# Holding GpSimd's gathers away from the slot products of a DLRM interaction kernel

## Chip, cores and metric

One NeuronCore of a Trainium2 chip. The metric is the device time of one execution in microseconds; the kernel before takes 124.73 us (median of 3 runs, 124.36 to 125.06).

## The reference, cut to what matters

512 samples, 26 embedding tables (1000 to 125000 rows of 128 floats) and one dense vector of 128 floats per sample. Per sample there are 27 slots (dense and 26 table rows); all 351 products of two different slots, with the dense vector twice, go through a three-layer MLP.

```python
e = jnp.stack([tbl_0[ids[:, 0]], ..., tbl_25[ids[:, 25]]], axis=1)
combined = jnp.concatenate((dense_features[:, None, :], e), axis=1)
interactions = jnp.einsum('bfd,bgd->bfg', combined, combined)
interactions_flat = interactions[:, iu, ju]          # 351 pairs, iu < ju
z = jnp.concatenate((dense_features, interactions_flat), axis=1)
h = jnp.concatenate([z, dense_features], axis=1)
h = jnp.maximum(h @ W_top1 + b_top1, 0.0)            # 607 -> 512
h = jnp.maximum(h @ W_top2 + b_top2, 0.0)            # 512 -> 256
y = h @ W_top3                                       # 256 -> 1
```

## The kernel before, in words

**Two ways to look up.** The 11 smallest tables are loaded whole into SBUF, and TensorE looks their rows up by multiplying with 0/1 masks (`look_up_first`, `look_up`, lines 321 to 365). The other 15 tables stay in HBM: GpSimd fetches their rows with indirect DMAs, one per table and tile of 128 samples, so 4 x 15 = 60 gathers (line 313), each of 128 rows of 512 bytes. The buffer `emb` holds two tiles. Gathers of tiles 1 and 2 fill it; those of tiles 3 and 4 take the places of tiles 1 and 2, once TensorE has transposed what was there (`s_tr`).

**The order of the gathers.** They go out one after the other, tile by tile. GpSimd does nothing else then. The function `hold(t, i)` (line 283) puts a wait ahead of gather `i` of tile `t`, `t` counted from 0; in this text tiles are counted from 1, as the loop over `p` does, and gathers of a tile from 0 to 14. Groups 0 to 3 of a tile (`GROUPS`) are its gathers 0 to 3, 4 to 7, 8 to 11 and 12 to 14, and each group has a semaphore (`s_gather`).

**The loop.** After the lookups, TensorE runs `Fori(1, TILES + 1)` over the tiles. What it does in iteration `p`, in program order:

- slot products, first half (`products`, line 408): for each of 16 column sets and each of 4 quarters of the array one 27 x 27 product of `xT` with itself, in float32. The profile shows two matmul records and two weight loads for each product, so 128 matmul records a half;
- `turn_next(p, (0,))`: transposes of group 0 of tile `p + 1` (line 374), 4 records; in iteration 1 also `dense_part` (line 414);
- slot products, second half, at whose end `s_prod` is incremented;
- for `p` over 1 the last layer of the tile before (`result`, line 445) and `dense_part`; then `turn_next(p, (1,))`, the transposes of group 1;
- `turn_pairs` (line 421) and the first layer (line 414), with VectorE's and ScalarE's rearranging of the products in between (lines 585 to 596 and 693 to 696);
- `turn_next(p, (2, 3))`, the transposes of groups 2 and 3, 7 records, then the second layer (line 504, 16 records).

Each transposed group is packed into `xT` by VectorE or ScalarE (lines 515 and 619), and the next iteration's products wait for that (`s_ready`). TensorE works through this order strictly: while it waits for a group of gathers, everything listed behind it waits too.

```python
                products(range(MATMULS // 2))
                turn_next(p, (0,))
                with nc.tensor.If(p < 2):
                    dense_part(slice(0, P), (0, 1))
                products(range(MATMULS // 2, MATMULS)).then_inc(s_prod, 1)
```

Of the kernel before, what the change touches and what calls it, by code (L numbers as in the profile page):

```python
# [46 lines left out]

QUADS = 4
MATMULS = P // QUADS


HALF = (SLOTS - 1) // 2
# [18 lines left out]
def build(nc, dense_t, ids, spread_ids, pair_ids, other_ids, resident, gathered, weights, out):  # L71
# [5 lines left out]
    first_step = [sum(n_rows[p[0]] for p in PAIRS[:b]) for b in range(len(PAIRS) + 1)]  # L77
# [7 lines left out]
    with ExitStack() as ctx:  # L85
        def sb(name, shape, dt=F32):
            return ctx.enter_context(nc.sbuf_tensor(name, shape, dt))

        def sem(name):
            return ctx.enter_context(nc.semaphore(name))  # L90
# [14 lines left out]
        known = sb("known", [D, 1 + RESIDENT, BATCH])  # L105
        xT = sb("xT", [D, MATMULS, QUADS, SLOT_PITCH])
        inter_s = sb("inter_s", [P, SLOTS * (ROW_PITCH + 1) + 1])
# [10 lines left out]

        prod = ctx.enter_context(nc.psum_tensor("prod", [P, MATMULS, SLOT_PITCH], F32))
        half_bank = [prod[:, h * MATMULS // 2:(h + 1) * MATMULS // 2, :].rearrange("p j g -> p (j g)")  # L120
                     for h in range(2)]
# [31 lines left out]
        s_used = sem("s_used")  # L153
# [7 lines left out]
        s_tr = sem("s_tr")  # L161
        s_pack = [sem(f"s_pack{g}") for g in range(NG)]
        s_prod = sem("s_prod")
        s_blk = sem("s_blk")
        s_wrap = sem("s_wrap")
        s_pick = [sem(f"s_pick{k}") for k in range(K_TILES)]
# [2 lines left out]
        s_l1 = sem("s_l1")  # L169
# [73 lines left out]
        def rows(t, c):  # L243

            return emb[:, t % 2 * GATHERED + c, :]

        def w1_pairs(k):
            return w_sb[0:K_PAIRS, W1P + k * HID1:W1P + (k + 1) * HID1]
# [26 lines left out]
        @block.gpsimd  # L275
        def _(pool):
            nc.gpsimd.memset(ident[:], 0.0).then_inc(s_zero, 1)
            pool.wait_ge(s_zero, 1)
            nc.gpsimd.affine_select(out=ident[:], in_=ident[:], compare_op=ALU.not_equal, fill=1.0, base=0,
                                    pattern=[[-1, P]], channel_multiplier=1).then_inc(s_ident, 1)  # L280
            pool.wait_ge(s_ids, 16)

            def hold(t, i):


                if (t, i) == (1, 0):
                    pool.wait_ge(s_used, first_step[2])
                if (t, i) == (1, 8):
                    pool.wait_ge(s_used, first_step[3] + 2)
                if (t, i) == (2, 0):  # L290
                    pool.wait_ge(s_used, first_step[4] + 3)
                if (t, i) == (2, 6):
                    pool.wait_ge(s_used, first_step[5] + 3)
                if (t, i) == (2, 10):
                    pool.wait_ge(s_prod, 1)
                if (t, i) == (3, 0):
                    pool.wait_ge(s_l1, 2)
                if (t, i) == (3, 4):
                    pool.wait_ge(s_prod, 2)
                if (t, i) == (3, 9):  # L300
                    pool.wait_ge(s_l1, 4)
                if (t, i) == (3, 13):
                    pool.wait_ge(s_prod, 3)

            for t in range(TILES):
                for g, (first, n) in enumerate(GROUPS):
                    if t >= 2:

                        pool.wait_ge(s_tr, NG * (t - 2) + g + 1)
                    for c in range(first, first + n):  # L310
                        hold(t, c)
                        i = t * GATHERED + c
                        nc.gpsimd.indirect_dma_start(  # L313
                            out=rows(t, c), out_offset=None, in_=gathered[c],
                            in_offset=bass.IndirectOffsetOnAxis(ap=ids_sb[:, i:i + 1], axis=0),
                        ).then_inc(s_gather[t % 2][g], 16)

        @block.tensor
        def _(pe):
# [83 lines left out]
            def products(some):  # L403

                for i in some:
                    for q in range(QUADS):
                        x = xT[:, i, q, 0:SLOTS]
                        mm = nc.tensor.matmul(prod[SLOT_PITCH * q:SLOT_PITCH * q + SLOTS, i, 0:SLOTS], x, x,  # L408
                                              start=True, stop=True)
                return mm  # L410
# [12 lines left out]
            def dense_part(samples, some):  # L423
                for n in some:
                    layer1(n, w1_sum, known[:, 0, samples], False)
# [39 lines left out]
            with nc.tensor.Fori(1, TILES + 1) as p:  # L465


                pe.wait_ge(s_ready, 2 * p)

                products(range(MATMULS // 2))  # L470
                turn_next(p, (0,))
                with nc.tensor.If(p < 2):
                    dense_part(slice(0, P), (0, 1))
                products(range(MATMULS // 2, MATMULS)).then_inc(s_prod, 1)
                samples = bass.ds((p - 1) * P, P)
                with nc.tensor.If(p > 1):

                    result(p - 1)
                    dense_part(samples, (0, 1))
                turn_next(p, (1,))  # L480

                pe.wait_ge(s_kept_last, 1)
                pe.wait_ge(s_y, p)
                turn_pairs(p, 0)
                dense_part(samples, (2, 3))
                pe.wait_ge(s_pair[0], p)
                first_pairs((0, 1))
                turn_pairs(p, 1)
                turn_pairs(p, 2)
                first_pairs((2, 3))  # L490
                for n in range(HID1 // P):
                    for k in range(1, K_TILES):
                        if n == 0:
                            pe.wait_ge(s_pair[k], p)
                        mm = layer1(n, w1_pairs(k), pairs[0:K_PAIRS, k, :], k == K_TILES - 1)
                    if n % 2:
                        mm.then_inc(s_l1, 1)
                turn_next(p, (2, 3))
                for half in range(2):
                    pe.wait_ge((s_h1_act, s_h1_dve)[half], p)  # L500
                    for m in range(HID2 // P):
                        for c in (2 * half, 2 * half + 1):
                            first = W2 + c * HID2 + m * P
                            mm = nc.tensor.matmul(l2_bank[m][:, 0:P], w_sb[:, first:first + P], h1[:, c, :],  # L504
                                                  start=(c == 0), stop=(c == HID1 // P - 1))
                        if half:
                            mm.then_inc(s_l2, 1)
# [3 lines left out]
        def _(dve):  # L511
# [66 lines left out]
            for t in range(TILES):  # L578
# [5 lines left out]
                for rows in (slice(0, K_ROWS), slice(K_ROWS, SLOTS)):  # L584
                    nc.vector.transpose(blocks[:, rows, 0:MATMULS],  # L585
                                        prod[:, :, rows].rearrange("p j g -> p g j")).then_inc(s_blk, 1)
# [188 lines left out]
```

## Time and profile before

| | before |
|---|---|
| runs, median (lowest to highest) | 124.73 us (124.36 to 125.06) |
| span of the profiled execution, first to last instruction | 123.0 us |
| median of the runs less that span | 1.73 us |
| TensorE matmul busy | 104.2 us (85%) |
| GpSimd busy | 65.7 us (53%), of it the 60 gathers 65.0 us |
| chain that ended last | PE 83%, issue 13%, DVE 2%, ACT 1% |
| line 408, idle just before its matmuls | 14.7 us, of it "issue" 14.2 us |

The profiled execution's own time is given as its span alone. How to read it: the span is cut into engine busy time; a busy share is no bound by itself. "Issue" is time in which an engine waited for nothing that the profile shows. "PEclk" is the clock that TensorE was granted, as a share of 2.4 GHz.

### The profile page before, as it was taken

The page shows a single profiled execution, that of the slowest core. Times are in us where ns is not written, and L with a number is a line of the kernel's source. Part 1 is how long each engine was busy: PE and PEld are TensorE (multiplying, and loading weights), DVE is VectorE, ACT ScalarE, POOL GpSimd, SP SyncE. Part 2 cuts the span into 40 slices and gives each one's busy share as a digit, 9 for nine tenths or more (in the row PEclk, how much of TensorE's full clock was granted, in tenths as well). Part 3 has the DMA queues.
Part 4 walks back from the last instruction along what each step waited for, and adds up shares of the span by engine and source line. Part 5 has one row for each costly group of instructions (what it writes and reads, how often), then busy time and mean ns, then how long its engine had stood idle before and what let it go on. Part 6 is the DMA issues. An engine that isn't in the chain of part 4 may idle for free.

```text
span 123.0 us, 3436 instructions
## 1 busy us (share of the span) xinstructions
PE 104.2 (85%) x1516; PEld 87.9 (71%) x1516; DVE 65.4 (53%) x110; ACT 48.1 (39%) x81; POOL 65.7 (53%) x66
## 2 busy tenths in 40 slices
PE   6999999999999999962178996289995299998993
PEld 6787888888888888831067895177992278996991
DVE  2599999999899996820001742105540106451411
ACT  4542979197794931300000462002541102730321
POOL 3887888579878887877500887503778305000000
PEclk9999999999999999999555999756999558999999
DMA  3799999999211112121200111200112100000000
GB/s 57 236 400 365 402 398 408 410 392 368 80 43 45 45 43 48 44 63 43 64 5 5 43 43 43 64 0 0 45 43 64 43 0 20 23 0 0 0 0 1
DMA packets 3949, 13.51 MB, mean 110 GB/s; under 512 B 1315, under 2 KB 1317, under 8 KB 3302
## 3 DMA queue, kind: packets, MB, share of 16 engines
q1 hardware_dynamic: 2018, 9.48, 20.5%
q0 software_dynamic: 1920, 3.94, 11.2%
q8 instruction: 4, 0.07, 0.2%
q14 instruction: 3, 0.02, 0.1%
q10 hardware_dynamic: 4, 0.00, 0.0%
HBM read 13.42 MB, written 0.00 MB: 109 GB/s over the span
## 4 chain that ended last, share of the span: by engine, by line
PE 83%; issue 13%; DVE 2%; ACT 1%
PE bank L365 17%; PE prod L408 13%; PE bank L414 13%; PE prod L365 12%; PE bank L374 7%; PE bank L504 6%; PE prod L433 4%; PE bank L321 4%; PE bank L325 3%; PE bank L445 2%; DVE inter_s L585 1%; PE bank L438 1%; PE prod L421 1%; PE bank L421 0%; DVE xT L575 0%
## 5 line engine op out<-in xcount | busy, mean ns | idle before, releaser
L313 POOL DMA_INDIRECT emb<-in_tbl,ids_sb x60 | 65.0, 1083 | 38.3 <-PE prod L408 19.3
L522 DVE TENSOR_SCALAR mask<-ids_h,ids_sb 128x1024 fp32r<-128x1024 int16 (+1 forms) x48 | 31.5, 699 | 2.2 <-issue 0.8
L408 PE MATMUL prod<-xT 128*27 128x27 f32 x1024 | 16.8, 215 | 14.7 <-issue 14.2
L408 PEld LDWEIGHTS prod<-xT 128*27 128x27 f32 x1024 | 13.6, 128 | 18.8 <-issue 17.4
L585 DVE STREAM_TRANSPOSE inter_s<-prod 128x288 f32<-128x288 f32 (+1 forms) x8 | 4.6, 611 | 26.3 <-PE prod L408 26.3
L365 PE MATMUL bank<-mask,high 128*128 128x512 f32 x46 | 15.2, 393 | 0.0
L365 PE MATMUL bank<-mask,low 128*128 128x512 f32 x46 | 15.0, 390 | 0.0
L414 PE MATMUL bank<-pairs,w_sb 117*128 117x128 f32 x96 | 12.7, 282 | 0.1
L414 PEld LDWEIGHTS bank<-pairs,w_sb 117*128 117x128 f32 x96 | 11.6, 191 | 0.7 <-ACT pairs L696 0.5
L531 DVE TENSOR_TENSOR low<-table,high 128x1024 fp32r<-128x1024 f32 (+1 forms) x9 | 11.7, 1301 | 0.0
L374 PE MATMUL bank<-ident,emb 128*128 128x128 f32 x60 | 10.5, 310 | 0.9 <-issue 0.9
L635 ACT CAST high<-table 128x1024 fp32r<-128x1024 f32 (+1 forms) x9 | 9.7, 1132 | 2.6 <-PE bank L325 2.6
L365 PE MATMUL prod<-mask,high 128*128 128x512 f32 x32 | 10.0, 395 | 0.0
L365 PEld LDWEIGHTS bank<-mask,low 128*128 128x128 f32 x46 | 8.6, 188 | 1.8
L365 PE MATMUL prod<-mask,low 128*128 128x512 f32 x32 | 9.9, 390 | 0.0
L693 ACT COPY pairs_s<-inter_s 128x117 f32<-128x117 f32 x8 | 2.3, 291 | 19.2 <-DVE inter_s L585 17.4
L365 PEld LDWEIGHTS bank<-mask,high 128*128 128x128 f32 x46 | 8.5, 188 | 1.7
L374 PEld LDWEIGHTS bank<-ident,emb 128*128 128x128 f32 x60 | 8.0, 160 | 1.8 <-issue 1.3
L711 ACT COPY y_row<-bank 1x128 f32<-1x128 f32 x4 | 1.0, 254 | 19.3 <-PE bank L445 19.3
L504 PE MATMUL bank<-h,w_sb 128*128 128x128 f32 x64 | 8.0, 278 | 0.0
L504 PEld LDWEIGHTS bank<-h,w_sb 128*128 128x128 f32 x64 | 7.5, 192 | 0.2 <-issue 0.2
L611 DVE TENSOR_SCALAR h<-bank,ids_sb 128x128 f32<-128x128 f32 x4 | 1.4, 351 | 11.3 <-remote 8.7
(55 smaller groups left out, 118.1 us busy)
## 6 DMA issues: line engine op xcount, KB each, us to landing
table<-in_resident SPq DMA_DIRECT2D x3, 1024.0 KB
w_sb<-in_weights SPq DMA_DIRECT2D x1, 1792.0 KB
table<-in_resident SPq DMA_DIRECT2D x1, 1280.0 KB
table<-in_resident SPq DMA_DIRECT2D x4, 256.0 KB
emb<-in_tbl,ids_sb POOLq DMA_INDIRECT x60
ids_h<-in_other_ids SPq DMA_DIRECT2D x1, 896.0 KB
table<-in_resident SPq DMA_DIRECT2D x1, 640.0 KB
ids_h<-in_pair_ids SPq DMA_DIRECT2D x1, 256.0 KB
```

The lines of the kernel that those rows point to most:

```text
L313: nc.gpsimd.indirect_dma_start(out=rows(t, c), out_offset=None, in_=gathered[c], in_offset=bass.IndirectOffsetOnAxis(ap=ids_sb[:, i:i + 1] ...
L321: nc.tensor.matmul(looked(r), split(high, r)[:, k * D:(k + 1) * D], made(k)[:, r, :], start=(k == 0), stop=False)
L365: mm = nc.tensor.matmul(looked(r), split(part, r)[:, k * D:(k + 1) * D], made(step)[:, r % 2, :], start=(k == 0 and part is high), stop=(k ...
L374: mm = nc.tensor.transpose(group_bank(g)[:, i * P:(i + 1) * P], rows(t, first + i), ident[:])
L408: mm = nc.tensor.matmul(prod[SLOT_PITCH * q:SLOT_PITCH * q + SLOTS, i, 0:SLOTS], x, x, start=True, stop=True)
L414: return nc.tensor.matmul(l1_bank[n // 2][:, (n % 2) * P:(n % 2 + 1) * P], weights[:, n * P:(n + 1) * P], x, start=(weights is w1_sum and ...
L433: nc.tensor.matmul(half_bank[1][:, 0:WARM_COLUMNS], warm, warm[:, 0:WARM_COLUMNS], start=True, stop=True)
L504: mm = nc.tensor.matmul(l2_bank[m][:, 0:P], w_sb[:, first:first + P], h1[:, c, :], start=(c == 0), stop=(c == HID1 // P - 1))
L522: nc.vector.tensor_scalar(made(step)[:, 0:n, :], ids_h[:, 2 * b:2 * b + n, :], col_sb[:, row:row + 1], None, ALU.is_equal).then_inc(s_mask, 1)
L531: nc.vector.tensor_tensor(split(low, r), raw(r), split(high, r).bitcast(F32), ALU.subtract).then_inc(s_low, 1)
L585: nc.vector.transpose(blocks[:, rows, 0:MATMULS], prod[:, :, rows].rearrange("p j g -> p g j")).then_inc(s_blk, 1)
L635: nc.scalar.copy(split(high, r), raw(r)).then_inc(s_high, 1)
```

## The change

Five of the nine waits of `hold` go, three come, and one more semaphore, `s_quiet`, is incremented by TensorE once per iteration, when 4 of the 16 column sets of the second half are done (32 of its 128 matmul records). Gathers 4 to 10 of tile 3 go out after that point of iteration 1, gathers 11 to 14 of tile 3 and 0 to 3 of tile 4 after that point of iteration 2, and gathers 4 to 14 of tile 4 after that point of iteration 3.

```diff
+STIR = MATMULS // 2 + 4
...
+        s_quiet = sem("s_quiet")
...
-                if (t, i) == (2, 6):
-                    pool.wait_ge(s_used, first_step[5] + 3)
-                if (t, i) == (2, 10):
-                    pool.wait_ge(s_prod, 1)
-                if (t, i) == (3, 0):
-                    pool.wait_ge(s_l1, 2)
+                if (t, i) == (2, 4):
+                    pool.wait_ge(s_quiet, 1)
+                if (t, i) == (2, 11):
+                    pool.wait_ge(s_quiet, 2)
                 if (t, i) == (3, 4):
-                    pool.wait_ge(s_prod, 2)
-                if (t, i) == (3, 9):
-                    pool.wait_ge(s_l1, 4)
-                if (t, i) == (3, 13):
-                    pool.wait_ge(s_prod, 3)
+                    pool.wait_ge(s_quiet, 3)
...
-                products(range(MATMULS // 2, MATMULS)).then_inc(s_prod, 1)
+                products(range(MATMULS // 2, STIR)).then_inc(s_quiet, 1)
+                products(range(STIR, MATMULS)).then_inc(s_prod, 1)
```

GpSimd's instructions keep their order, only their waits move. The first place is tile 3's gathers 4 to 14 (in_tbl_7 is gather 4, in_tbl_23 gather 14; `s_tr` is the wait for the transposes that free the buffer, `s_used` one for a lookup step). Before:

```order
L313 DMA emb<-in_tbl_7,ids_sb 128x128 [waits s_tr]
L313 DMA emb<-in_tbl_9,ids_sb 128x128
L313 DMA emb<-in_tbl_11,ids_sb 128x128 [waits s_used]
L313 DMA emb<-in_tbl_14,ids_sb 128x128
L313 DMA emb<-in_tbl_17,ids_sb 128x128 [waits s_tr]
L313 DMA emb<-in_tbl_18,ids_sb 128x128
L313 DMA emb<-in_tbl_19,ids_sb 128x128 [waits s_prod]
L313 DMA emb<-in_tbl_20,ids_sb 128x128
L313 DMA emb<-in_tbl_21,ids_sb 128x128 [waits s_tr]
L313 DMA emb<-in_tbl_22,ids_sb 128x128
L313 DMA emb<-in_tbl_23,ids_sb 128x128
```

The same gathers on GpSimd in the change:

```order
L311 DMA emb<-in_tbl_7,ids_sb 128x128 [waits s_quiet,s_tr]
L311 DMA emb<-in_tbl_9,ids_sb 128x128
L311 DMA emb<-in_tbl_11,ids_sb 128x128
L311 DMA emb<-in_tbl_14,ids_sb 128x128
L311 DMA emb<-in_tbl_17,ids_sb 128x128 [waits s_tr]
L311 DMA emb<-in_tbl_18,ids_sb 128x128
L311 DMA emb<-in_tbl_19,ids_sb 128x128
L311 DMA emb<-in_tbl_20,ids_sb 128x128 [waits s_quiet]
L311 DMA emb<-in_tbl_21,ids_sb 128x128 [waits s_tr]
L311 DMA emb<-in_tbl_22,ids_sb 128x128
L311 DMA emb<-in_tbl_23,ids_sb 128x128
```

Seven gathers stand between the first wait for `s_quiet` and the second. The second place is tile 4's gathers 4 to 14 on GpSimd, before:

```order
L313 DMA emb<-in_tbl_7,ids_sb 128x128 [waits s_prod,s_tr]
L313 DMA emb<-in_tbl_9,ids_sb 128x128
L313 DMA emb<-in_tbl_11,ids_sb 128x128
L313 DMA emb<-in_tbl_14,ids_sb 128x128
L313 DMA emb<-in_tbl_17,ids_sb 128x128 [waits s_tr]
L313 DMA emb<-in_tbl_18,ids_sb 128x128 [waits s_l1]
L313 DMA emb<-in_tbl_19,ids_sb 128x128
L313 DMA emb<-in_tbl_20,ids_sb 128x128
L313 DMA emb<-in_tbl_21,ids_sb 128x128 [waits s_tr]
L313 DMA emb<-in_tbl_22,ids_sb 128x128 [waits s_prod]
L313 DMA emb<-in_tbl_23,ids_sb 128x128
```

And in the change:

```order
L311 DMA emb<-in_tbl_7,ids_sb 128x128 [waits s_quiet,s_tr]
L311 DMA emb<-in_tbl_9,ids_sb 128x128
L311 DMA emb<-in_tbl_11,ids_sb 128x128
L311 DMA emb<-in_tbl_14,ids_sb 128x128
L311 DMA emb<-in_tbl_17,ids_sb 128x128 [waits s_tr]
L311 DMA emb<-in_tbl_18,ids_sb 128x128
L311 DMA emb<-in_tbl_19,ids_sb 128x128
L311 DMA emb<-in_tbl_20,ids_sb 128x128
L311 DMA emb<-in_tbl_21,ids_sb 128x128 [waits s_tr]
L311 DMA emb<-in_tbl_22,ids_sb 128x128
L311 DMA emb<-in_tbl_23,ids_sb 128x128
```

Before, the wait at gather 4 was for the products of iteration 2; now it is for a point in those of iteration 3, and all eleven gathers stand behind that one wait.

## Rows read from the trace of the kernel before

**Rows 1.** The span and mean granted clock of the core.

```profile
core 0: 123.0 us, clock 0.902
```

**Rows 2.** The page's costliest groups: line 408's matmuls, and the idle time before them.

```profile
L408 PE MATMUL prod<-xT 128*27 128x27 f32 x1024 | 16.8, 215 | 14.7 <-issue 14.2
```

**Rows 3.** Windows of the slot products: stretch, length, PE busy (records), PEclk, DMA share, GB/s.

```profile
53.70:62.22 8.52, 2.37 (x57) 0.75 0.19 48
62.22:63.31 1.09, 1.09 (x72) 0.50 0.00 0
65.53:67.22 1.69, 1.64 (x128) 0.50 0.00 0
75.00:80.33 5.33, 1.56 (x40) 0.82 0.19 50
80.33:81.62 1.29, 1.29 (x90) 0.50 0.00 0
82.67:84.31 1.64, 1.64 (x129) 0.50 0.00 0
92.81:97.94 5.13, 1.36 (x31) 0.76 0.20 51
110.15:113.17 3.02, 2.47 (x256) 1.00 0.00 0
```

**Rows 4.** Windows behind each tile's products; busy: PE, PEld, DVE, ACT, POOL; clock, DMA.

```profile
67.22:75.00 7.78, 7.22 (x65) 6.92 (x69) 4.81 (x10) 3.97 (x9) 6.00 (x6) 0.94 0.16 44
84.31:92.81 8.50, 8.50 (x66) 7.41 (x64) 4.80 (x10) 4.32 (x10) 6.18 (x6) 0.95 0.15 40
102.31:110.15 7.84, 7.84 (x74) 7.35 (x75) 4.71 (x10) 4.50 (x11) 1.89 (x2) 1.00 0.06 17
113.17:123.00 9.83, 7.89 (x60) 6.52 (x59) 2.93 (x8) 2.42 (x9) 0.00 (x0) 0.99 0.00 0
```

**Rows 5.** The chain that ended last, in order of time: start, us, what.

```profile
53.70 0.52 PE prod L408 x38
54.23 0.18 issue
...
81.62 1.05 PE bank L374 x4
...
110.15 1.20 PE prod L408 x83
111.35 0.55 issue
111.90 1.27 PE prod L408 x83
```

**Rows 6.** GpSimd's timeline: start, us, and in brackets the idle time before.

```profile
51.88 0.94 POOL L313 DMA_INDIRECT emb<-in_tbl,ids_sb  x1 [0.30 <-issue]
...
59.37 0.94 POOL L313 DMA_INDIRECT emb<-in_tbl,ids_sb  x1 [0.30 <-issue]
67.48 0.94 POOL L313 DMA_INDIRECT emb<-in_tbl,ids_sb  x1 [7.17 <-PE prod L408]
...
75.59 0.94 POOL L313 DMA_INDIRECT emb<-in_tbl,ids_sb  x1 [0.30 <-issue]
...
78.08 0.94 POOL L313 DMA_INDIRECT emb<-in_tbl,ids_sb  x1 [0.30 <-issue]
```

**Rows 7.** The chain in iteration 3 behind its products.

```profile
103.47 0.44 PE bank L374 x4
...
107.60 0.77 PE bank L374 x7
108.36 1.79 PE bank L504 x16
```

**Rows 8.** Windows around the fall and the return of the granted clock in iteration 2.

```profile
78.00:79.00 1.00, 0.08 (x4) 0.10 (x4) 0.00 (x0) 0.00 (x0) 0.92 (x1) 0.70 0.24 66
...
85.00:86.00 1.00, 1.00 (x8) 0.86 (x8) 0.93 (x3) 0.60 (x3) 0.89 (x1) 0.89 0.00 0
```

## The prediction, made before the changed kernel ran

> **What bounds the kernel now.** I read the span first [rows 1]: 123.0 us, 1.73 below the median of the runs (124.73). I take 1.73 as what lies around every span. The costliest groups come next: line 408's 1024 matmul records are busy for 16.8 us, yet TensorE sat idle for 14.7 us just ahead of them, 14.2 of it "issue", with nothing in the profile that it waited for [rows 2]. The windows show where [rows 3]. A half of the products is 128 records. Iteration 4's two halves took 3.02 us in all, with no DMA traffic at all. Iteration 1 ran only 57 records in its first 8.52 us, iteration 2 only 40 in 5.33, iteration 3 only 31 in 5.13; each of these stretches has a DMA share of 0.19 or 0.20. The remaining records of the same halves, and all the second halves, ran without a break, and their rows have no DMA traffic.
>
> Only gathers were under way then. GpSimd's last one before the pause started at 59.37 and took 0.94, so it ended at 60.31, and TensorE ran freely from 62.22; in iteration 2 the last one ended at 79.02, and TensorE was free from 80.33, which is 1.31 later [rows 3, 6]. So it is the transfer, which ends behind the instruction, that matters. At the start of each stretch some records pass unhindered: 38 in iteration 1 before the first gap, at 54.23 [rows 5]. Something of that size stands ready ahead of the array; after it, the other 19 of the 57 took 8.0 us, 2.4 a microsecond. The long matmuls between the products, 66 records in 8.50 us with six gathers on GpSimd, show no idle time [rows 4]; that is 7.8 a microsecond, so what starves the products is not a fixed rate, and I only take from the rows when it starts and when it ends.
>
> The gaps cost twice. The clock was 1.00 in iteration 4's products and 0.50 behind each starved stretch [rows 3]: with a gap-ridden TensorE it fell near 78.7 (0.70 over 78 to 79) and came back near 85 (0.89 over 85 to 86) [rows 8].
>
> **The change, part by part.** All times are in the profiled span.
>
> *Iteration 1.* Products start at 53.70 as before. Tile 3's gather 3 (51.88 plus 0.94) goes as before, gather 4 is held. Its transfer is over by 54.1 (1.31 behind its end), just when the first gap came, so I leave 0.3 us of stall: first half 1.20 [rows 5] + 0.3 = 1.5. Between the halves stand four transposes and four `dense_part` records, 2.22 us from 63.31 to 65.53 at half clock [rows 3]; at full clock half of that, and 0.3 for the branches, which cost 0.55 where they stood alone [rows 5]: 1.4. Second half 1.27. Products end at 57.9 where it was 67.22. The rest of the iteration, 7.78 us at clock 0.94 [rows 4], is kept at 7.8: iteration 2 starts at 65.7 instead of 75.00.
>
> *First release.* 32 records (0.32 us) into the second half, at 56.9; GpSimd starts 0.25 later, 57.2 (before, 67.22 to 67.48). Before, the seventh gather behind such a release started at 75.59, 8.11 later, and took 0.94 [rows 6]. So seven gathers end at 57.2 + 9.05 = 66.2, and TensorE is free of them at 67.5. The remaining 96 records of the half need 1.0 us, in which no transfer has begun yet; I price that at nothing. The cover is the 38 records that stood ready, and the first transfer; if it fails, see the third rival.
>
> *Iteration 2.* It starts at 65.7 and the batch reaches until 67.5: a stall of 1.8 us is left where it was 5.3. The rest of the half is 0.9 at full clock (90 records took 1.29 at half [rows 3]): 68.4. Group 0's transposes (1.05 at half clock [rows 5], 0.5 at full) and 0.5 of branches: 69.4. Second half 1.27: 70.7, where it was 84.31. The rest was 8.50, its beginning at half clock; I take 7.9, near iteration 3's 7.84 [rows 4]: iteration 3 starts at 78.6. Group 3 of tile 3 ends with the fourth gather of the second batch, which lands about when TensorE asks for it; it costs nothing or a few tenths.
>
> *Second release.* At 69.7, GpSimd from 70.0; eight gathers are 9.05 + 1.25 = 10.3 (1.25 is 0.94 and the 0.30 before it [rows 6]), so 80.3, TensorE free at 81.6.
>
> *Iteration 3.* 3.0 us of stall from 78.6 to 81.6, 0.9 for what is left, 1.0 between the halves: second half from 83.5, third release at 83.8.
>
> *Third release: the bill.* Eleven gathers from 84.1: 9.05 + 4 x 1.25 = 14.05, so the last ends at 98.1 and has landed at 99.3 (I take 1.2 behind the end, near the 1.31 of above). They are tile 4's, and iteration 3 itself transposes them. Before, TensorE turned group 1 at 103.47, some 2.8 us behind the start of the second half (100.67), and groups 2 and 3 at 107.60, 6.9 behind [rows 7]. Now group 1 lands 7 us behind, so TensorE stands still there for about 4.6 us, and everything queued behind it (pairs, first layer) with it; then groups 2 and 3 keep it until 99.3, 15.8 behind. The first wait lies inside the second, so the price is 15.8 less 6.9, some 9 us. What comes next runs at half clock after such idling: the last three transposes 0.7 and the second layer 3.6 where it was 1.79 [rows 7], so iteration 4 starts at 103.6 (at full clock 101.4).
>
> *Iteration 4.* 3.02 plus 0.3 for what is still at half clock, then 9.83 [rows 4]: span 116.7. With 1.73 the time is **118.5 us**, 6.2 less than the median.
>
> In the sum: iteration 1 gives 9.3, iterations 2 and 3 (starved 5.3 and 5.1, doubled clock time with them) give 4.3 and 5.0 before the third release, the third release takes 9 and the clock behind it some 2 to 3 more.
>
> A rule of the Trainium skill bears on what starves TensorE. Iteration 4's first half, which stands behind the same backward jump as the others, took 1.20 us without a gap [rows 5]. The page "Runtime: NRT & Kernel Launch", section "Instruction fetch mechanics", says that a taken branch to a target outside the small window of fetched instructions forces a fetch before execution goes on. By it each iteration's beginning would be starved whatever GpSimd does, the trace speaks against it as the whole cause, and the sum would be that of the first rival.
>
> **The rivals.**
>
> *The stalls come from the loop's jump, not from the gathers.* For it: all three stalls are in first halves, and no second half had gathers beside it. Against: iteration 4, and the ends of the stalls, which follow the last gather's end by 1.31 and 1.91. Then iterations 1 to 3 stay as they are, and the third release falls at 101.1 in the old time: landed at 101.1 + 0.25 + 14.05 + 1.2 = 116.6, second layer done at 120.9 where it was 110.15. With 0.3 more at half clock that is 11 us on top: 135.8. Chance 0.08.
>
> *The batches' tails starve the products as long as before, or not at all.* If a freed TensorE needs as long as it did (6.62 us from 75.00 to 81.62 [rows 3]) in iterations 2 and 3, the third release comes 6.6 later: 125.1, no change. 0.08. If the tails do no harm, because 38 and more records stand ready and the jump alone matters little, the third release comes 4.3 earlier: 114.2. 0.08.
>
> *The early release starves the rest of its own half.* This one decides if the supply turns thin as soon as GpSimd begins, not with the first transfer, and fewer than the remaining 96 records stand ready (38 did at 53.70). Then the second halves of iterations 1 to 3 wait for their batches: iteration 1 ends its products at 68.0, iteration 2 (a clean first half; release at 78.3; eight gathers) at 90.7, iteration 3 (release at 101.1) at 117.2, and with 7.84 + 3.02 + 9.83 the span is 137.9: 139.6. No gather was started in the midst of products before, so no row excludes it; against it speaks that the release from starvation follows the transfer's end. 0.08.
>
> **How the numbers follow.** The forecast has 0.68. Its own range is about 115.5 to 121: full clock behind the third release takes 2 off, half clock in the products of iterations 2 and 3 adds about 2. Leaving out the first and third rival (0.16) and half of the long tails (0.04), the range is 114.0 to 124.0. A measurement can tell 0.5%, 0.6 us, from no change. Faster: 0.68 + 0.08 + 0.02 of the long tails = 0.78; same 0.06; slower 0.16.
>
> **What would show it.** Right: line 408's "issue" idle falls from 14.2 to about 5; iteration 1's products in some 4 us at clock 1.00; a last gather ending near 98; TensorE idle by 4 to 5 us before group 1's transposes and by 3 to 4 before group 3's in iteration 3, for DMA landings. Wrong: gaps of line 408 with no gather in flight, or in second halves; no idle time in iteration 3 behind its products; eleven gathers that take much more or less than 14 us.

## The result and the profile after

The change takes 130.89 us (median of 4 runs, 130.43 to 131.96); the kernel before, run on the same chip, 124.9 us (124.36 to 125.56). The ratio is 1.056, with a 95% interval of 1.045 to 1.066: the change is slower, where 118.5 us had been forecast. All ratios below are to the kernel before on the same chip and compare the fast runs of each kernel (those within 1.5% of its fastest), so where half or more of a kernel's runs were slower, as in e1, e7 and e8, the ratio lies below the quotient of the medians.

The page of the change: span, busy times, the granted clock in 40 slices, and two of the costliest groups (line 406 is what was line 408, line 372 what was 374).

```profile
span 129.0 us, 3436 instructions
PE 106.2 (82%) x1516; PEld 90.2 (70%) x1516; DVE 65.4 (51%) x110; ACT 48.1 (37%) x81; POOL 66.3 (51%) x66
PEclk9999999999999999999689975556999955599999
L406 PE MATMUL prod<-xT 128*27 128x27 f32 x1024 | 13.1, 194 | 9.0 <-issue 8.6
L372 PE MATMUL bank<-ident,emb 128*128 128x128 f32 x60 | 9.9, 296 | 6.3 <-DMA emb<-in_tbl,ids_sb 4.9
```

The "issue" idle ahead of the products fell from 14.2 us [rows 2] to 8.6; it has not gone. Line 372's transposes now wait 4.9 us for gathers, and the clock falls three times, around 62 to 65 us, 76 to 89 and 103 to 113. The windows show where it is now (stretch, length; busy PE, PEld, DVE, ACT, POOL; clock, DMA share, GB/s). Products and rest of iterations 1 to 3 alternate; the last row is iteration 4's products.

```profile
54.03:59.35 5.32, 3.76 (x264) 3.33 (x264) 0.47 (x1) 0.00 (x0) 0.98 (x2) 1.00 0.02 5
59.35:70.80 11.45, 9.05 (x66) 8.19 (x69) 4.70 (x10) 4.31 (x10) 6.36 (x6) 0.85 0.14 42
70.80:83.39 12.59, 5.66 (x262) 4.03 (x262) 0.35 (x1) 0.00 (x0) 7.54 (x8) 0.69 0.12 36
83.39:94.30 10.91, 10.08 (x73) 9.21 (x75) 4.70 (x10) 4.59 (x11) 0.00 (x0) 0.73 0.02 6
94.30:97.62 3.32, 3.06 (x261) 2.70 (x260) 0.35 (x1) 0.00 (x0) 0.02 (x1) 1.00 0.00 0
97.62:116.10 18.48, 11.70 (x75) 10.80 (x77) 4.71 (x10) 4.66 (x11) 11.08 (x11) 0.72 0.13 39
116.10:119.15 3.05, 2.50 (x257) 2.31 (x258) 0.35 (x1) 0.00 (x0) 0.00 (x0) 1.00 0.00 0
```

By stages, against the boundaries in [rows 3, 4] (before, then after; us):

| | products | rest |
|---|---|---|
| up to iteration 1 | | 53.70, 54.03 |
| iteration 1 | 13.52, 5.32 | 7.78, 11.45 |
| iteration 2 | 9.31, 12.59 | 8.50, 10.91 |
| iteration 3 | 9.50, 3.32 | 7.84, 18.48 |
| iteration 4 | 3.02, 3.05 | 9.83, 9.85 |

The products of iterations 1 and 3 give 14.4 us. Iteration 2's products take back 3.3, and the three rests 16.7. With 0.4 for the start and iteration 4 that is 6.0, the difference of the spans.

Iteration 2's products are the surprise. TensorE's timeline of the change there (start, us, what, and in brackets the idle time before):

```profile
72.52 0.93 PE L406 MATMUL prod<-xT 128*27 128x27 f32 x84
73.84 0.27 PE L406 MATMUL prod<-xT 128*27 128x27 f32 x6 [0.39 <-issue]
74.57 0.27 PE L406 MATMUL prod<-xT 128*27 128x27 f32 x6 [0.46 <-issue]
...
83.19 0.20 PE L406 MATMUL prod<-xT 128*27 128x27 f32 x1 [1.12 <-issue]
```

GpSimd's timeline, the first gather of each batch and the last of the second:

```profile
58.07 0.94 POOL L311 DMA_INDIRECT emb<-in_tbl,ids_sb  x1 [4.91 <-PE prod L406]
...
73.28 0.94 POOL L311 DMA_INDIRECT emb<-in_tbl,ids_sb  x1 [6.04 <-PE prod L406]
82.01 0.95 POOL L311 DMA_INDIRECT emb<-in_tbl,ids_sb  x1 [0.30 <-issue]
97.60 0.94 POOL L311 DMA_INDIRECT emb<-in_tbl,ids_sb  x1 [14.65 <-PE prod L406]
```

The second batch began at 73.28. At 73.45 TensorE stopped with 84 of the half's 128 records through, and then got one to six records every 0.72 us or 1.44 us until the batch was over: 44 records in 9.9 us. By the records' starts it had stopped sooner: all 84 had begun when GpSimd's first record starts, and the 0.17 us are those in flight. The other two batches began later in their halves. Against the first record of the half, batch 1 began 1.26 us later. The last 24 records came after a pause of 1.08 us, but this pause begins 0.16 us ahead of GpSimd's start, and iteration 1's second half pauses behind its 104th or 105th record in runs with no gather anywhere near too: 0.56 us in e3, 0.66 in e1, 0.71 to 0.92 in e4, e7 and e8. So at most half a microsecond of the 1.08 is the gather's; what makes this pause wasn't looked for. Batch 3 began 1.26 later too and found the half all but done: all 128 records passed in one piece of 1.30 us. Batch 2 began 0.76 later. GpSimd's wait for `s_quiet` was its only one there, while in iterations 1 and 3 a wait for `s_tr` stands beside it (the order of instructions shown with the change).

The second thing is in VectorE's timeline. The instruction that waits for the end of the products:

```profile
60.85 1.15 DVE L584 STREAM_TRANSPOSE inter_s<-prod 128x288 f32<-128x288 f32 x2 [6.35 <-PE prod L406]
84.88 1.15 DVE L584 STREAM_TRANSPOSE inter_s<-prod 128x288 f32<-128x288 f32 x2 [13.69 <-PE prod L406]
```

The products had ended at 59.35 and 83.39, so VectorE went on 1.5 us late each time; in iteration 3 it was 2.07 us (97.62 to 99.69). Before, it started 0.02 behind the end at 67.22.

### The profile page after: what moved, and what is told of

Same layout as the page of the kernel before. It is cut to its first block, busy times and chain, and to the rows that moved or that the text cites. A ratio compares the mean times of both kernels' runs of the same rounds, so it can differ in the third digit from the quotient of the medians.

```text
span 129.0 us, 3436 instructions
## 1 busy us (share of the span) xinstructions
PE 106.2 (82%) x1516; PEld 90.2 (70%) x1516; DVE 65.4 (51%) x110; ACT 48.1 (37%) x81; POOL 66.3 (51%) x66
## 4 chain that ended last, share of the span: by engine, by line
PE 80%; issue 13%; POOL 2%; DMA 2%; DVE 1%; ACT 1%; POOLq 0%
PE bank L412 16%; PE bank L363 16%; PE prod L363 11%; PE prod L406 9%; PE bank L372 6%; PE bank L503 6%; PE prod L431 4%; PE bank L319 4%; PE bank L323 3%; POOL emb L311 2%; DMA emb<-in_tbl,ids_sb 2%; PE bank L443 2%; PE prod L419 1%; PE bank L436 1%; PE bank L419 1%
## 5 line engine op out<-in xcount | busy, mean ns | idle before, releaser
L406 PE MATMUL prod<-xT 128*27 128x27 f32 x1024 | 13.1, 194 | 9.0 <-issue 8.6
L412 PE MATMUL bank<-pairs,w_sb 117*128 117x128 f32 x96 | 16.6, 332 | 2.0 <-issue 2.0
L406 PEld LDWEIGHTS prod<-xT 128*27 128x27 f32 x1024 | 10.7, 104 | 10.6 <-issue 9.2
L412 PEld LDWEIGHTS bank<-pairs,w_sb 117*128 117x128 f32 x96 | 15.4, 243 | 2.7 <-issue 2.6
L372 PE MATMUL bank<-ident,emb 128*128 128x128 f32 x60 | 9.9, 296 | 6.3 <-DMA emb<-in_tbl,ids_sb 4.9
L372 PEld LDWEIGHTS bank<-ident,emb 128*128 128x128 f32 x60 | 7.5, 151 | 7.3 <-DMA emb<-in_tbl,ids_sb 5.1
L595 DVE COPY pairs<-prod 117x128 f32<-117x128 f32 x4 | 1.2, 292 | 13.2 <-remote 7.7
L412 PE MATMUL bank<-known,w_sum 128*128 (+1 forms) x32 | 7.2, 364 | 0.0
```

Source lines behind the costliest of these rows:

```text
L372: mm = nc.tensor.transpose(group_bank(g)[:, i * P:(i + 1) * P], rows(t, first + i), ident[:])
L412: return nc.tensor.matmul(l1_bank[n // 2][:, (n % 2) * P:(n % 2 + 1) * P], weights[:, n * P:(n + 1) * P], x, start=(weights is w1_sum and ...
```

## The experiments

Kernels sent together ran on one chip, and the chips were not alike. Of the five used here the kernel before took 125 us on two, as in the runs that the prediction was made from, and 107 us on three. I call these the **107 chips** and the **125 chips**. E1 to E8 ran on 125 chips, e9 to e17 on 107 chips.

**Releases at the end of the products.** `s_quiet` and `STIR` go, and the same three batches wait for `s_prod`:

```diff
                 if (t, i) == (2, 4):
-                    pool.wait_ge(s_quiet, 1)
+                    pool.wait_ge(s_prod, 1)
                 if (t, i) == (2, 11):
-                    pool.wait_ge(s_quiet, 2)
+                    pool.wait_ge(s_prod, 2)
                 if (t, i) == (3, 4):
-                    pool.wait_ge(s_quiet, 3)
+                    pool.wait_ge(s_prod, 3)
```

> The change with its three releases moved from 32 records into the second half to the end of the products (s_prod 1, 2, 3). Theory A (a gather starves the products from the moment GpSimd starts on it, and iteration 2 lost about 10 us that way because 44 records were still to come): line 406's idle time falls from 9.0 us to under 3, iteration 2's second half takes 1.3 us instead of 10.8, and part of that comes back since the second batch, released 1 us later, now reaches into iteration 3's first half; span 119 to 123 us, so 121 to 125. Theory B (the loop's second iteration is starved by something else, such as its code): iteration 2's second half stays at about 10 us and the time at 131.

Measured: 122.64 us (120.80 to 124.37), ratio 0.966 (0.959 to 0.973); by the medians it is 0.980. The trace is that of a run of 124.37 us, span 122.5. Windows: iteration 2's products and rest, and iteration 3's rest.

```profile
67.62:74.25 6.63, 4.52 (x261) 3.84 (x262) 0.35 (x1) 0.00 (x0) 1.89 (x2) 0.82 0.12 30
74.25:83.81 9.56, 8.46 (x73) 7.49 (x75) 4.80 (x10) 4.23 (x10) 7.18 (x7) 0.95 0.17 41
...
89.25:109.70 20.45, 11.11 (x74) 10.28 (x78) 4.72 (x10) 4.69 (x11) 11.08 (x11) 0.75 0.15 36
```

The second halves of iterations 2 and 3 run clean, iteration 1's but for the pause of 0.66 us; VectorE starts 0.02 to 0.03 us behind their ends, and iteration 1's rest is 7.79 us again. The batches' tails now starve the first halves of iterations 2 and 3. Holding the gathers out of the products is worth 3.4% on such a chip, or 2.0% by the medians; releasing them earlier, in the products, is slower than before.

**The third hold undone.** The wait ahead of tile 4's gather 4 goes, so the 19 gathers behind the second release follow one another.

```diff
-                if (t, i) == (3, 4):
-                    pool.wait_ge(s_quiet, 3)
```

> The change without its third wait: tile 4's gathers 4 to 14 follow the second batch at once (19 gathers in one go from iteration 2's products). Theory A: the 10.7 us that iteration 3's rest grew by (18.5 for 7.84) are gone, iteration 3's first half is starved again by 3 to 6 us, iteration 2's second half as in the change; span about 123, time 125 plus or minus 1.5. Theory B (the third hold is not what costs; TensorE is slow there for another reason): the rest of iteration 3 stays above 15 us.

Measured: 136.44 us (134.83 to 138.29), ratio 1.086 (1.077 to 1.095). The third release's bill did go, and iteration 3's products ran clean. But iteration 2's rest took 26.24 us, and the time is 11 us over the 125 expected. The products had ended at 84.06; VectorE, which waits for that, went on at 101.06, 17.0 us late and 3.4 behind the end of the last gather (97.63):

```profile
90.41 0.37 PE L370 MATMUL bank<-ident,emb 128*128 128x128 f32 x1 [1.32 <-issue]
...
101.06 1.15 DVE L582 STREAM_TRANSPOSE inter_s<-prod 128x288 f32<-128x288 f32 x2 [28.98 <-remote]
```

Until 92.9 even TensorE's 128 x 128 matmuls came one to three at a time, with pauses of 0.35 to 1.32 us (the first row is one); then it waited 9.12 us for ScalarE's line 690, which waits for that VectorE instruction. I had not priced that.

**No late gathers at all.** Tile 3's gathers 4 to 14 and tile 4's are left out, and their waits are set so that TensorE turns what stands in the buffer; all other work stays.

```diff
+                        if (t, c) >= (2, 4):
+                            continue
                         hold(t, c)
```

> The kernel of e1 with the last 26 gathers left out (tile 3's 4 to 14 and all of tile 4; tiles 3 and 4 then use rows of tiles 1 and 2). Theory A (only the gathers starve the products and delay the rest): each half of the products takes 1.2 to 1.3 us, all four rests 7.6 to 8 us, clock 1.00 throughout, span 100 to 102 us. Theory B (loop jump or code fetch starve the first halves): gaps of some us in the first halves remain, span over 108.

Measured: 102.36 us, span 100.5, clock 1.00. Windows: iteration 1's rest, iteration 2's and iteration 3's products.

```profile
57.89:65.66 7.77, 7.11 (x66) 6.76 (x70) 4.72 (x10) 4.34 (x10) 0.00 (x0) 1.00 0.01 2
65.66:68.65 2.99, 2.99 (x261) 2.68 (x261) 0.35 (x1) 0.00 (x0) 0.00 (x0) 1.00 0.00 0
76.57:79.78 3.21, 3.05 (x261) 2.70 (x262) 0.35 (x1) 0.00 (x0) 0.00 (x0) 1.00 0.00 0
```

Every first half from iteration 2 on stands behind the loop's jump as before, and none pauses at all. On a 125 chip the late gathers cost 123.0 - 100.5 = 22.5 us. One pause remains, in iteration 1's second half, with no gather since 52.40:

```profile
55.83 1.07 PE L406 MATMUL prod<-xT 128*27 128x27 f32 x105
57.45 0.36 PE L406 MATMUL prod<-xT 128*27 128x27 f32 x23 [0.56 <-issue]
```

**One probe of each kind.** As e3, with one gather into a scratch buffer begun amid iteration 2's first half, five GpSimd memsets in iteration 3's, and one load by SyncE from iteration 4's first half on; TensorE releases each 32 records into the half (`s_probe`).

```diff
+            pool.wait_ge(s_probe, 2)
+            nc.gpsimd.indirect_dma_start(
+                out=scratch[:, 0, :], out_offset=None, in_=gathered[0],
+                in_offset=bass.IndirectOffsetOnAxis(ap=ids_sb[:, 0:1], axis=0),
+            ).then_inc(s_scr, 16)
+            pool.wait_ge(s_scr, 16)
+            pool.wait_ge(s_probe, 3)
+            for s in range(5):
+                nc.gpsimd.memset(scratch[:, 2 + s, :], 0.0)
```

> The kernel of e3 with one probe each, released 32 records into a first half: one gather in iteration 2, five memsets of 128x128 on GpSimd in iteration 3 (about 1 us), one 64 KB load issued by SP in iteration 4. Theory A1 (writing the gather's descriptors on GpSimd or its transfer is what starves): a gap of 1 to 2.5 us in iteration 2, none in 3 and 4. Theory A2 (any work on GpSimd): gaps in 2 and 3. Theory A3 (any DMA transfer): gaps in 2 and 4. Where the gap begins against the start of the gather tells whether the instruction or the transfer does it.

Measured: 104.77 us. The timeline of TensorE (line 423 is the products) and GpSimd:

```profile
66.60 0.93 PE L423 MATMUL prod<-xT 128*27 128x27 f32 x84
67.36 0.94 POOL L324 DMA_INDIRECT scratch<-in_tbl,ids_sb  x1 [14.19 <-PE prod L423]
67.92 0.27 PE L423 MATMUL prod<-xT 128*27 128x27 f32 x6 [0.40 <-issue]
68.66 0.54 PE L423 MATMUL prod<-xT 128*27 128x27 f32 x38 [0.47 <-issue]
...
78.82 1.30 PE L423 MATMUL prod<-xT 128*27 128x27 f32 x128
79.43 0.79 POOL L331 MEMSET scratch<- 128x128 f32 x5 [11.13 <-PE prod L423]
```

One gather is enough: the last record before the gap ended 0.17 us behind its start (all 84 had begun by that start), and the supply was free again at 68.66, 0.36 us behind the instruction's end (68.30). Its transfer ran from 69.0 to 69.25 and held nothing up. So the instruction starves TensorE, not the transfer, and GpSimd's memsets do nothing of the kind; nor did SyncE's load, whose transfer ran beside iteration 4's second half. What in the instruction does it stays open.

**The second release half a microsecond later.** One more wait, long fulfilled, ahead of the one that counts, so that batch 2 begins as late in its half as batches 1 and 3:

```diff
                 if (t, i) == (2, 11):
+                    pool.wait_ge(s_tr, NG + 1)
                     pool.wait_ge(s_quiet, 2)
```

> The change with one more wait, satisfied long before (s_tr), ahead of the wait for s_quiet 2, so that the second release carries two waits as the first and the third do. Theory C (in the change GpSimd starts 0.37 us behind the second release but 0.75 to 0.87 behind the first and third, because a gather with two waits is only taken up after the release; that half microsecond decides whether 44 records or none are still to come): the second batch starts about 1.2 us behind the start of iteration 2's second half, that half takes 1.3 to 2.5 us instead of 10.8, span 119 to 122, time 121 to 124. Theory D (iteration 2 is starved for a reason of its own): time stays at 131.

Measured: 129.26 us (128.63 to 130.27), ratio 1.039 (1.025 to 1.052), where 121 to 124 us had been expected; the interval overlaps that of the change (1.045 to 1.066). GpSimd's, VectorE's and ScalarE's timelines in iteration 2:

```profile
73.83 0.95 POOL L312 DMA_INDIRECT emb<-in_tbl,ids_sb  x1 [6.60 <-PE prod L407]
...
75.91 1.15 DVE L585 STREAM_TRANSPOSE inter_s<-prod 128x288 f32<-128x288 f32 x2 [4.68 <-remote]
...
80.93 0.27 ACT L696 COPY pairs<-bank 117x128 f32<-117x128 f32 x1 [3.25 <-remote]
```

The half did run clean: 128 records in 1.29 us, ending at 73.85. But the signal of that end reached VectorE 2.06 us late, while TensorE itself had gone on with twelve longer matmuls; ScalarE went on 3.4 us behind the transpose it needs (line 420, which ended at 77.57), and the rest took 18.83 us. In e1 the batch began 0.26 us behind the end of the products, and the rest took 9.56. These two rests differ by 9.3 us, with the batch starting 0.02 us before the end of the products in one and 0.26 us behind it in the other. That the placing alone makes all of the 9.3 isn't shown: nothing between was tried, and iteration 1's rest, behind a batch that began amid its products too, took 11.6 us in e5, not 18.8. My expectation had only the clean half. The padding gave 9.5 us back in iteration 2's products (3.07 for 12.59) and lost 7.9 in its rest.

**The opposite: single waits at the other two releases.** The waits for `s_tr` at gather 4 of tiles 3 and 4, which order nothing there, go:

```diff
-                    if t >= 2:
+                    if t >= 2 and (t, g) not in ((2, 1), (3, 1)):
```

> The change without the s_tr waits at gather 4 of tiles 3 and 4, which are satisfied long before (s_quiet implies them), so that all three releases carry a single wait. Theory C: the first and third batches start half a microsecond earlier, iteration 1's second half is starved until its seven gathers are done (about 8 us more) and iteration 3's too, part of which lies inside the wait for its eleven gathers; span over 134. Theory D: no difference, 131.

Measured: 143.14 us (141.46 to 143.45), ratio 1.145 (1.130 to 1.161). Windows of the three second halves from their first record:

```profile
57.52:68.14 10.62, 3.54 (x129) 2.58 (x130) 0.00 (x0) 0.00 (x0) 6.62 (x7) 0.78 0.18 46
79.49:90.09 10.60, 3.62 (x129) 2.47 (x129) 0.00 (x0) 0.00 (x0) 7.56 (x8) 0.71 0.17 43
102.19:112.79 10.60, 3.75 (x130) 2.38 (x129) 0.00 (x0) 0.00 (x0) 7.56 (x8) 0.77 0.18 43
```

Now all three are starved alike, each with 84 records through before the first pause. Taking one long-fulfilled wait away at each of two releases turned two nearly clean halves into starved ones, at 12 us: this shows that the placing alone made iteration 2's products differ.

**Can the bill of the third release be made smaller?** Three kernels. E7 is e1 with e6's edit. E8 is e7 with iteration 3's second layer ahead of `turn_next(p, (2, 3))`:

```diff
+                with nc.tensor.If(p == TILES - 1):
+                    second_layer(p)
+                    turn_next(p, (2, 3))
...
```

> The kernel of e1 (released at the end of the products) without those two s_tr waits. Theory C: the first and third batch start 0.5 us earlier with no product left to starve, so up to 1 us less than e1: about 121.5 us. Theory D: same as e1.

> The kernel of e7, and in iteration 3 the second layer (line 504's 16 records) runs ahead of the transposes of groups 2 and 3, inside the wait for the gathers instead of behind it. If the last gather's landing is what bounds, the 1.8 to 3.2 us of the second layer leave the path and about 1 us of packing takes their place: 1 to 2 us less than e7, so 119.5 to 121. If not, no difference.

Measured: e7 122.01 us (120.13 to 124.31), ratio 0.968 (0.953 to 0.982), not told apart from e1: released at the end of the products, half a microsecond makes no difference that these runs can tell. E8 124.55 us (121.74 to 125.85), ratio 0.980 (0.972 to 0.988), by the medians 0.996: the second layer began only at 103.12, behind late signals, and took 3.78 us at half clock. No gain over e7.

E9 is e7 with matmuls of `ident`, 5 and 3, ahead of groups 1 and 3 in iteration 3 so that TensorE doesn't idle there; their results are overwritten. E10 has e8's edit too.

```diff
+                            if g in (1, 3):
+                                with nc.tensor.If(p == TILES - 1):
+                                    stay_warm(g, 5 if g == 1 else 3)
```

> The kernel of e7 and, in iteration 3, five 128x512 float32 matmuls of no use ahead of the wait for group 1's gathers and three ahead of the wait for group 3's (about 0.9 us each at full clock), into the bank that the transposes then overwrite. If the half clock behind the third release costs what iteration 3's second layer shows (3.2 us in e1, 2.1 in e7, against 1.8 at full clock, and the first layer's records likewise), the time falls by 1 to 2 us to 119 to 121. If these matmuls are themselves starved by the gathers and come in late, the time stays or rises.

> The kernel of e8 with the same matmuls. In e8 the second layer, drawn ahead of the last transposes, ran at half clock (3.8 us) and began late, so that nothing was left of its gain. With the clock kept, 1 to 2 us less than e9, so 118 to 120; if the signals that it waits for are what is late, no better than e9.

Measured, on a 107 chip: e9 117.86 us, ratio 1.113 (1.105 to 1.121); e10 116.49 us, ratio 1.099 (1.091 to 1.107). In iteration 3 the clock did stay at 1.00 and the second layer took 1.79 and 2.05 us, but before ran in 106.79 there. So these two say nothing about a 125 chip, where they were not tried.

**Loads by SyncE in place of gathers.** E3 with twelve loads by SyncE, one behind the other, from iteration 2's first half on.

> The kernel of e3 (no late gathers) with twelve 64 KB loads issued by SP, one behind the landing of the other, from 32 records into iteration 2's products on, so that they lie beside the products of iterations 2 and 3. If transfers as such starve the products, gaps of 0.4 us and more appear there as beside gathers. If it is GpSimd's own part in a gather, as the single probe suggests (gap from 0.16 us behind its start, free again before its transfer), there are none, and the span is that of e3 within 1 us.

Measured: 103.17 us, span 101.4, no pause in the products of iterations 2 to 4. On that chip gathers hardly starve them either, so it says little.

**The four kernels side by side on 107 chips.** E12 is the kernel before, e13 the change, e14 repeats e7, e15 and e16 repeat e9, e17 repeats e10; no edit is new.

> The kernel before, for its profile on this chip. If starvation by gathers belongs to the chip: either 125 us with 14 us of idle time before line 408, as first, or about 107 us with under 3. Anything in between would speak for a state that comes and goes within a chip.

> The change. On a chip that starves: 131 us, 5% slower than before. On one that doesn't: the products are free anyway, and only the third release's wait for eleven gathers is left, so about 118 us against 107, 10% slower.

> The kernel of e7. On a chip that starves: 122 us, 3% faster than before. On one that doesn't: 117 to 119 us, 10% slower, since GpSimd's idle time during the products is all it has.

> The kernel of e9 (5 and 3 matmuls of no use in iteration 3's waits). On a chip that starves: 119 to 121 us, a little less than e14. On one that doesn't: the same as e14.

> The kernel of e9. On a starving chip (before at 125 us): 119 to 121 us if the half clock behind the third release is what costs, 122 as e7 if the late signals are. On the other kind (before at 107 us): 118 us again.

> The kernel of e10. On a starving chip: 1 us under e16 if the second layer's signals come in time, else no less. On the other kind: 116.5 us again.

Measured:

| | us | ratio (95% interval) |
|---|---|---|
| e12, before | 106.49 | |
| e13, the change | 115.27 | 1.080 (1.058 to 1.101) |
| e14, as e7 | 117.49 | 1.100 (1.084 to 1.115) |
| e15, as e9 | 117.70 | 1.105 (1.089 to 1.121) |
| e16, as e9 | 118.12 | 1.107, from 106.69 before |
| e17, as e10 | 116.19 | 1.094 (1.088 to 1.100) |

The kernel before on such a chip: its products' group, and its first halves of iterations 2 and 3 with gathers beside them.

```profile
L408 PE MATMUL prod<-xT 128*27 128x27 f32 x1024 | 12.2, 193 | 2.5 <-issue 1.6
```

```profile
68.13:69.87 1.74, 1.62 (x130) 1.38 (x130) 0.35 (x1) 0.00 (x0) 1.43 (x2) 1.00 0.23 64
79.58:81.31 1.73, 1.63 (x129) 1.32 (x128) 0.35 (x1) 0.00 (x0) 1.17 (x2) 1.00 0.14 38
```

Gathers run at the same pace there (0.94 us and 0.30 between), but a half beside them takes 1.7 us, where iteration 2's first half took 6.6 on a 125 chip (75.00 to 81.62 [rows 3]). VectorE went on 0.04 to 0.28 us behind the end of each iteration's products in e12 and e13, so the late signals are missing there too. The spans of e12 and e11 differ by 104.7 - 101.4 = 3.3 us, about what late gathers cost there, against 22.5. There is little to win by holding them, and the bill stays. The rest of iteration 3 in e13 took 17.67 us, and TensorE waited twice for gathers there:

```profile
88.95 1.12 PE L372 MATMUL bank<-ident,emb 128*128 128x128 f32 x4 [5.08 <-DMA emb<-in_tbl,ids_sb]
97.99 0.55 PE L372 MATMUL bank<-ident,emb 128*128 128x128 f32 x3 [2.58 <-DMA emb<-in_tbl,ids_sb]
```

In e12 the same stretch takes 7.90 us. So on a 107 chip the loss of the change is this one bill, 9.8 us, less 1.3 elsewhere in the span. E15 against e14, on one chip, shows that holding the clock at 1.00 gained nothing there: 117.70 for 117.49 us.

## Why the prediction was wrong

The span was to be 116.7 us and was 129.0. Step by step, predicted and measured:

| step | predicted | measured | off by |
|---|---|---|---|
| start of iteration 1 | 53.7 | 54.03 | +0.3 |
| iteration 1, products | 4.2 | 5.32 | +1.1 |
| iteration 1, rest | 7.8 | 11.45 | +3.7 |
| iteration 2, products | 5.0 | 12.59 | +7.6 |
| iteration 2, rest | 7.9 | 10.91 | +3.0 |
| iteration 3, products | 6.2 | 3.32 | -2.9 |
| iteration 3, rest | 18.8 | 18.48 | -0.3 |
| iteration 4 | 13.1 | 12.90 | -0.2 |

**The step that failed** is in the first release: "The remaining 96 records of the half need 1.0 us, in which no transfer has begun yet; I price that at nothing", resting on "So it is the transfer, which ends behind the instruction, that matters". E4 shows that the instruction starves the supply from its start on, and that its transfer harms nothing. In iteration 2 the 44 records that were left took 9.9 us, where my 1.0 us for 96 makes about 0.5. What I had read as 38 records standing ready gave no cover amid a half: all 84 records that passed had begun when the gather did. At the start of a half some do pass while a batch is under way, 38, 25 and 17 in the kernel before:

```profile
74.93 0.64 PE L408 MATMUL prod<-xT 128*27 128x27 f32 x25
92.81 0.33 PE L408 MATMUL prod<-xT 128*27 128x27 f32 x17
```

So a stock of that size can stand ready after a wait, and I took it to be there at all times. I inferred the transfer from where the stalls ended, 1.31 and 1.91 us behind the last instruction's end [rows 3, 6], and took that as saying where they begin, which those rows don't show. The one gather of e4 let go 0.36 us behind its end. My third rival named this mechanism and got 0.08. It came true in part, since it held only in iteration 2, for the half microsecond that a second wait costs GpSimd; with all three releases alike it costs 143.14 us (e6), near the 139.6 of that rival. And what I had called evidence against it, that the release from starvation follows the transfer's end, was the same inference again.

**A cost that nobody named**: signals arrive late. Where a batch begins at or before the end of the products, VectorE and ScalarE get TensorE's signals 1.5 to 3.4 us late, and 17.0 late in e2. The kernel before had it too, off its path: its second layer ended at 92.81 ahead of iteration 3, and VectorE went on 5.2 us later, 1.4 behind the last gather of the batch that starved the half:

```profile
97.98 0.35 DVE L611 TENSOR_SCALAR h<-bank,ids_sb 128x128 f32<-128x128 f32 x1 [5.73 <-remote]
```

By size, it makes most of the +3.7 in iteration 1's rest (a 1.5 us late start, a clock of 0.85 where it was 0.94, 2.4 us without a matmul) and 17 us of e2's 26.24. In iteration 2's rest, where no gather runs, it is the 1.5 us late start again and the half clock behind the starved products: 10.08 us of matmul at clock 0.73 for 8.50 at 0.95 [rows 4].

**Right**: the stalls come from the gathers. The first rival, the loop's jump, is dead: in e3 the products of iterations 2 to 4, behind the same jump, take 2.99 to 3.21 us. So the rule that the prediction cited, the Trainium skill, "Runtime: NRT & Kernel Launch", "Instruction fetch mechanics", does not bound this loop; in e3 no record behind a jump waits, and the pauses at the branches between the halves are below 0.6 us. The clock stayed at 1.00 in iteration 1's products. Their +1.1 us is for the most part the pause that e1 and e3 have too (0.56 and 0.66 us).

**Right in the number, in part by luck**: the bill of the third release, 18.48 us for 18.8. Its first wait came as written, 4.93 us for 4.6, and the eleven gathers took 14.2 us for 14.05. The second did not: TensorE never waited for the last gathers, where 3 to 4 us had been expected, and the second layer ran at full clock (1.79 us, not 3.6). In their place stood late signals to ScalarE and VectorE and a first layer at half clock:

```profile
109.98 3.57 PE L412 MATMUL bank<-pairs,w_sb 117*128 117x128 f32 x16 [1.82 <-issue]
113.38 0.93 PE L372 MATMUL bank<-ident,emb 128*128 128x128 f32 x7
```

The two kinds of cost came out alike. The tails of the batches did no harm in iteration 3's products (3.32 us for 6.2), but only because the starved second half of iteration 2 had absorbed its batch; in e1, where it had not, iteration 3's products took 5.44 us and iteration 2's 6.63, against my 6.2 and 5.0.

One line of the prediction doesn't fit its own times: the summary says that iterations 2 and 3 give 4.3 and 5.0 us ahead of the third release, but the times above it give 4.9 and 3.0. The 118.5 us don't rest on that line.

The gain of e1 is small because the bill of the third release stands in every version that holds the gathers.

No version beats the kernel before on both kinds of chip: e1 gives 3.4% on a 125 chip, and e14, e7's kernel, loses 10% on a 107 chip.

## What to carry to other kernels

Before placing a release amid dense work, find out when the harm begins, not only when it ends, and count how long the waiting engine takes to go on: here half a microsecond less at two releases cost 12 us (e6). Work that is held must still be paid behind its release: eleven gathers at 1.25 us ahead of a consumer 3 us away cost 9.8 to 12.6 us on either kind of chip (iteration 3's rest took 18.48 us in the change and 20.45 in e1, for 7.84; 17.67 in e13, for 7.90). And a stall for which the profile names no cause may belong to the chip at hand: measure on a second one before building on it.

## What the runs showed of the hardware

- **A gather instruction on GpSimd starves TensorE's shortest matmuls.** On 125 chips 44 records of the products took 9.9 us, where a half of 128 takes 1.27. Longer matmuls were not stopped in the kernel before (66 records at clock 0.95 in 8.50 us with six gathers beside [rows 4]), but they were where a batch ran on behind starved products: in e2 128 x 128 records came one to three at a time, with up to 1.32 us between. Memsets on GpSimd, the transfer itself and one load by SyncE did nothing (e4).
- **It also delays TensorE's signals**, by 1.5 to 3.4 us, and 17.0 us in e2, where a batch begins at or before the end of the products. Where it begins 0.26 us behind the end or later, that signal is on time (0.02 to 0.03 us, e1). On 107 chips it was 0.04 to 0.28 us (e12, e13).
- **Chips differ**: the same kernel took 125 us on some and 107 on others, with gathers of the same length. What makes them differ stays open. The one other difference that I saw is that pages from 107 chips give a landing time for the gathers (2.7 to 2.9 us where all 60 ran, 5.0 in e11) and those from 125 chips give none. What this means isn't known, and e4's single gather, on a 125 chip, does have one (2.6 us).
- **GpSimd's way out of a wait**: its first gather started 0.26 us behind the end of the products where it had one wait, 0.76 and 0.77 us where a second, fulfilled one stood beside it (e1).
- **The clock**: keeping TensorE busy with unused matmuls held it at 1.00 through iteration 3, and the second layer took 1.79 us (e9), not 3.2 to 3.8 (e1, e8); but the change and e7 took no more than 1.79 and 2.05 without them. What that is worth on a 125 chip was not tried.
